# A memset behind each row gather in a graph kernel with four layers

## What is computed

```python
def _L0_gnn_ref(A, X, W, b):
    scores = jnp.where(mask, -jnp.arange(N), -inf)
    vals, idx = jax.lax.top_k(scores, S)            # S = 25: the first 25 neighbours
    feats = jnp.where(valid[..., None], X[idx], -inf)
    agg = feats.max(axis=2)
    agg = jnp.where((degree <= S)[..., None], jnp.maximum(agg, 0.0), agg)
    return relu(concatenate([X, agg]) @ W + b)

x = _layernorm(x + _L0(adj, x, ...))
x = _layernorm(x + _L1(x, adj, ...))     # graph attention, softmax over neighbours
x = _layernorm(x + _L2(x, adj, ...))     # the same again with other weights
x = _layernorm(x + _L3(x, adj, ...))     # dense attention, two steps with tanh
```

## Time and profile before

| | |
|---|---|
| timed runs, median of 3 | 1908.94 us (1906.79 to 1909.59) |
| profiled execution, span | 2892.8 us |
| TensorE matmul busy | 1713.1 us (59%) |
| TensorE weight load busy | 1233.8 us (43%) |
| VectorE busy | 1366.6 us (47%) |
| ScalarE busy | 937.2 us (32%) |
| GpSimd busy | 1263.5 us (44%) |
| mean granted TensorE clock | 0.773 of full speed |

### The profile page before, as it was taken

How to read it: one execution, slowest core, us unless ns; L and a number is a source line. 1 busy time by engine, 2 the same in 40 slices (tenths; PEclk the granted TensorE clock), 3 DMA queues, 4 the chain that set the end, 5 groups by cost and what they waited for, 6 DMA issues and landing times.

```text
span 2892.8 us, 27186 instructions
## 1 busy us (share of the span) xinstructions
PE 1713.1 (59%) x8580; PEld 1233.8 (43%) x8580; DVE 1366.6 (47%) x3417; ACT 937.2 (32%) x1311; POOL 1263.5 (44%) x1310
## 2 busy tenths in 40 slices
PE   1655767535765457664574655656455564756778
PEld 0543554424543245343452434434343343533655
DVE  3663664334743347443464434544354544443642
ACT  1010533323433324233332342223432325223223
POOL 5376344455344453444454443544435444255000
PEclk9987777767887668776697766877678776788789
DMA  4221212222222222222232221222312222121001
GB/s 126 61 74 43 71 51 90 55 77 62 59 77 61 66 62 61 77 71 55 58 85 62 70 77 29 80 70 70 77 38 71 70 69 63 36 67 52 23 15 37
DMA packets 160697, 182.18 MB, mean 63 GB/s; under 512 B 106397, under 2 KB 123690, under 8 KB 160554
## 3 DMA queue, kind: packets, MB, share of 16 engines
q1 hardware_dynamic: 119594, 96.43, 12.2%
q0 software_dynamic: 40960, 83.97, 10.8%
HBM read 155.66 MB, written 4.19 MB: 55 GB/s over the span
## 4 chain that ended last, share of the span: by engine, by line
PE 36%; another core or an unknown queue 24%; issue 18%; DVE 12%; ACT 5%; DVEq 4%; DMA 1%; SPq 1%; ACTq 0%
PE big L917 5%; PE spare L817 5%; PE side L1015 4%; PE big L1032 4%; PE big L986 4%; DVEq L69 3%; PE big L843 2%; PE big L999 2%; DVE probs_t L1327 2%; DVE pooled L1204 1%; PE big L817 1%; PE big L908 1%; PE big L864 1%; ACT adj_less L536 1%
## 5 line engine op out<-in xcount | busy, mean ns | idle before, releaser
L508 POOL DMA_INDIRECT gathered<-in_x_dram,rows x1280 | 1259.0, 984 | 1410.7 <-DVE pooled L1205 616.7
L817 PE MATMUL spare<-hot,x_part 128*128 128x512 f32 x1088 | 305.8, 427 | 86.9 <-issue 58.2
L917 PE MATMUL big<-values,probs_t 128*128 128x129 f32 x1792 | 254.0, 299 | 117.8 <-issue 117.0
L917 PEld LDWEIGHTS big<-values,probs_t 128*128 128x128 f32 x1792 | 241.8, 214 | 130.7 <-issue 125.7
L817 PEld LDWEIGHTS spare<-hot,x_part 128*128 128x128 f32 x1088 | 216.0, 203 | 150.5 <-issue 107.2
L1204 DVE TENSOR_REDUCE pooled<-gathered 128x128 f32<-128x2688 f32 (+1 forms) x56 | 253.0, 4517 | 6.4 <-issue 6.4
L986 PE MATMUL big<-probs_t,values 128*128 128x512 f32 x256 | 132.2, 666 | 160.4 <-issue 152.4
L1393 DVE TENSOR_REDUCE neg_max<-big 128x1 f32<-128x1024 f32 x64 | 78.3, 1223 | 286.2 <-remote 182.8
L1015 PE MATMUL side<-recip_diag,work 128*128 128x128 f32 x1024 | 143.6, 296 | 116.7 <-ACT probs_t L679 54.5
L1015 PEld LDWEIGHTS side<-recip_diag,work 128*128 128x128 f32 x1024 | 134.3, 208 | 146.6 <-issue 120.0
L563 ACT ACTIVATE hot<-running,minus_count 128x2048 fp32r<-128x2048 bf16 x84 | 167.4, 1993 | 58.9 <-remote 58.7
(11 more groups left out here) (191 smaller groups left out, 2642.0 us busy)
## 6 DMA issues: line engine op xcount, KB each, us to landing
adj_in<-in_adj_dram SPq DMA_DIRECT2D x128, 512.0 KB
gathered<-in_x_dram,rows POOLq DMA_INDIRECT x1280
xs<-in_x_dram SPq DMA_DIRECT2D x8, 512.0 KB
out_dram<-xs SPq DMA_DIRECT2D x8, 512.0 KB
adj_t<-adj_bf SPq DMA_TRANSPOSE x64
packed_t<-group_bits SPq DMA_TRANSPOSE x28
w_sb<-in_L_gnn_W_dram SPq DMA_DIRECT2D x1, 128.0 KB
w_sb<-in_L_gnn_W_dram SPq DMA_DIRECT2D x2, 64.0 KB
```

The costliest lines, as they stand in the source:

```text
L508: (late_gathered if late else rows_gathered[t % RING]).raised_by(pool.indirect_dma_start(out=gathered[:, t % RING, k * C:(k + 1) * C], out ...
L817: last = nc.tensor.matmul(pick_bank(b, q), x_parts[part][:, m, :], hot[c][:, m % per, :], start=(m == 0 and part == 0), stop=(m == T - 1 a ...
L917: last = nc.tensor.matmul(heads[:, t, 0:C + 1], probs_t[:, j, t * P:(t + 1) * P], values[:, j, :], start=False, stop=(j == T - 1), skip_gr ...
```

## The change

A new SBUF tile `pause` holds 6 x 256 bf16 elements on each partition. Behind each gather k of a tile GpSimd writes zeros to 256 elements on 32 partitions of it: partitions 0, 32, 64 or 96 onwards by k % 4, in column block k // 4, so that no two memsets of a tile touch the same place. The last memset of a tile raises a new semaphore, `paused`, and each tile but the first waits ahead of its gathers until the last memset of the tile before has been written. Nothing reads `pause`. There is no drain between a gather and its memset.

```diff
--- before.py
+++ after.py
@@ -30,6 +30,7 @@
 GATHERED = (21, 21)
 GATHERED_FIRST = 13
 LATE = 6
+PAUSE = 256
 PICKED = (SAMPLES - GATHERED[0], SAMPLES - GATHERED[1])
 PICKS = PICKED[0] + PICKED[1]
 BY_DVE = (PICKED[0], PICKED[0] + 1)
@@ -210,6 +211,7 @@
         row_f = sb("row_f", [P, 2, GATHERED[0]])
         rows = sb("rows", [P, T, GATHERED[0]], U32)
         gathered = sb("gathered", [P, RING, GATHERED[0] * C])
+        pause = sb("pause", [P, -(-GATHERED[0] // 4), PAUSE], BF16)
         running = sb("running", [P, T, N // 2], BF16)
         hot = [sb(f"hot{c}", [P, T // CHUNKS, N // 2], F32R) for c in range(CHUNKS)]
         x_parts = [sb(f"x_part{i}", [P, T, C], F32R) for i in range(X_PARTS)]
@@ -306,6 +308,7 @@
                                 first=ring_tiles(i, T) * GATHERED_FIRST - (i == late_ring) * LATE)
                          for i in range(RING)]
         late_gathered = signal("late_gathered", LATE, 16)
+        paused = signal("paused", T)
         gathers_begun = ctx.enter_context(nc.semaphore("gathers_begun"))
         loads_begun = ctx.enter_context(nc.semaphore("loads_begun"))
         rows_pooled = signal("rows_pooled", T)
@@ -495,6 +498,8 @@
                                         pattern=[[step, P]], channel_multiplier=-step).then_inc(consts, 1)
 
             def gather(b, t):
+                if t or not (isinstance(b, int) and b == 0):
+                    pool.wait_ge(paused.sem, paused.at(b, t))
                 if t % 2 == 0:
                     pool.wait_ge(rows_ready.sem, rows_ready.at(b, t // 2 + 1))
                 if t >= RING:
@@ -508,6 +513,9 @@
                     (late_gathered if late else rows_gathered[t % RING]).raised_by(pool.indirect_dma_start(
                         out=gathered[:, t % RING, k * C:(k + 1) * C], out_offset=None, in_=x_rows,
                         in_offset=bass.IndirectOffsetOnAxis(ap=rows[:, t, k:k + 1], axis=0)))
+                    quarter = k % 4 * 32
+                    last = nc.gpsimd.memset(pause[quarter:quarter + 32, k // 4, :], 0.0)
+                paused.raised_by(last)
 
             for t in range(T):
                 gather(0, t)
```

## The result

| | timed median | runs |
|---|---|---|
| kernel before | 1907.87 us | 1903.70 to 1909.59 |
| changed kernel | 2234.13 us | 2231.94 to 2235.16 |

The ratio is 1.171, with a 95% interval of 1.1688 to 1.1732: 326 us slower. The forecast was 2016 us (1959 to 2065 us as the case's own range), so the direction was right and the size was not: 107 us forecast, 326 us measured. The measured time lies in the wide range (1915 to 2260 us) and near the rival in which every memset costs its full length, 2214 us.

The account below looks back on a forecast made before the run. GpSimd was taken as all but the bound, TensorE's chain right beside it. 1908.9 + 122 (memsets) + 30 (borders) - 45 (slack) = 2016 us; likeliest case 1959 to 2065 us, wide range 1915 to 2260 us.

Parts of the forecast that it names:

- the case's own range: Bounds of the likeliest case, in which one memset in four costs its full length: 1959 to 2065 us, chance 0.45.
- The head of the page and the earlier trace: Profiled span of 2892.8 us against 1908.94 us timed: the extra 984 us are other engines' stalls while gathers run.
- The budget of GpSimd's idle time: Timed window for gathers, 1667 to 1706 us, leaves GpSimd 25 to 107 us idle; 45 us taken as absorbing work.
- The memset: 1280 memsets behind gathers: full length 0.25 us for one quarter, floor 0.033 us for the rest, 122 us in all.
- the quarter: In the memset's price: only memsets on partitions of the part preparing gathers, 368 of 1280, cost their full 0.25 us.
- the volume written: In the memset's price: 32 x 256 elements priced like 128 x 64, 0.087 us each, 111 us in all.
- The gap: The 0.30 us between gathers on GpSimd: claimed to be the engine's own execution, unable to hide a memset.
- the full-length rival: Every memset between gathers costs its full 0.25 us, 320 us in all: 2214 us (2157 to 2263), chance 0.25.
- The border: At each tile's start, the wait for GpSimd's last memset costs 0.6 us; 50 borders counted, 30 us (15 to 38).
- Collisions with VectorE: Memsets and gathers meeting VectorE's `hot` comparison hold each other up: set at nothing, bound some 10 us.
- What would prove me wrong: Gather step 1.28 us behind three memsets, 1.50 us behind the fourth; wrong on price if the step doesn't grow.
- The rival "faster": Thinner gather bursts relieve starved engines: 79 us back at most, 1830 us; a third gives 1883 us; chance 0.05.

Follow-up runs that it names:

- the border's wait alone: Kernel before plus one one-element memset behind a tile's last gather and the wait for it ahead of the next tile: 1933.6 us, 1.012.
- warm borders: Changed kernel with the border's wait raised by an earlier memset, so met beforehand: 2203.6 us, 1.155 of kernel before; 2327 us, 0.787, where that takes 2956 us.

## Why the prediction failed, step by step

**The head of the page and the earlier trace rows.** That the profiled execution lost its 984 us to stalls that the timed runs don't have was right, and the profile of the kernel before without stalls confirms it. I had left open why. The runs show that it goes with the chip, or with its state at the time, and not with the kernel; what stalls there isn't shown. The trace names no releaser for much of it: ScalarE's waits on something that the profile can't name are 631 us in the profile ahead of the prediction and 196 us in the one without stalls.

**The budget of GpSimd's idle time.** It gave 25 to 107 us for the window from the first gather on; measured are 30.6 us. Its two ends, 1667 and 1706 us for that window, hold the measured 1697 us. This step carried the sign of the forecast, and it held. I took 45 us of the idle time as able to absorb work, and 20 us of the first wait for pooling as able to absorb nothing; there are only 30.6 us, of which 28.9 us went in the change and 13 us in the run with the border's wait alone, and 1.7 us were left. Mis-sized by 16 us.

**The memset.** This is the step that failed. "If GpSimd's partitions are served by separate parts of it" gave 122 us; measured are 278.5 us. Two reasons stood for the low price, the quarter and the volume written, and the runs refute both: 1.276 us a step on the lower partitions, on the upper ones, and on all 128. The plain reading of the earlier trace rows, 0.25 us each and 320 us in all, was on the page, with the note that no row shows a memset made cheaper by fewer partitions. I let an account of how the engine is divided overrule the nearest rows. The rule that stood beside it, of the Trainium skill's GPSIMD Engine Reference, Instruction dispatch, and Perfetto Trace Analysis, DMA Instruction, SWDGE, would make three of four memsets cheap; the measurement decides against that reading. The pages don't say that a core skips a memset whose partitions are another core's; I added that.

**The gap.** "Can the 0.30 us gap hide it? I say no" was wrong in part. Behind a gather comes 0.04 us, the memset's span, and 0.16 us: 0.20 us of gap in place of 0.30 us. Some 0.10 us of a memset's span is hidden, so 256 elements (0.304 us) cost 0.204 us, 128 elements (0.198 us) cost 0.097 us, and one element (0.094 us) costs nothing. With this, the full-length rival's 320 us becomes 261 us. The kernels with 64 elements hide more: a span of 0.166 us costs 0.026 us, since the memset begins at the gather's end and not 0.04 us behind it. Those three kernels write the same partitions every time. In the others the 0.04 us is also gone exactly where two memsets in a row have the same quarter, at the first memset of 63 tiles; with warm borders, where no two do, it is never gone. So part of the price seems to belong to moving on to other partitions; no run tested that by itself.

**The border.** 0.6 us each was forecast, 30 us in all. The gap is 0.84 us in place of 0.16 us, 0.68 us each, and the waits for the memset are 47.8 us. Right in mechanism, 18 us short, or 9 us net of the 0.16 us that stand there anyway. By the runs its worth is 31 us in the changed kernel and 26 us alone.

**Collisions with VectorE.** "I set it at nothing; the bound is some 10 us." The gathers' busy time grew by 29.9 us, some 6 us of it because every gather takes 0.950 us in place of 0.945 us, the rest by collisions; the memsets' grew by about 18 us. GpSimd, then VectorE, in the changed kernel:

```profile
1044.69 0.30 POOL L517 MEMSET pause<- 32x256 bf16 x1
1045.15 1.89 POOL L513 DMA_INDIRECT gathered<-in_x_dram,rows  x1 [0.16 <-issue]
1047.08 0.30 POOL L517 MEMSET pause<- 32x256 bf16 x1
1047.55 1.89 POOL L513 DMA_INDIRECT gathered<-in_x_dram,rows  x1 [0.16 <-issue]
...
1043.74 8.46 DVE L1335 SCALAR_TENSOR_TENSOR probs_t<-row_gain,col_gain,adj_t 128x1024 f32<-128x1024 f32 x7
```

A gather beside VectorE's products of probabilities takes 1.89 us here in place of 0.95, and the next one again. Seven of those products take 8.46 us, 1.20 us from one to the next; the gathers then begin at 1045.15 and 1047.55, 2.40 us apart, so each meets the train at the same point of a product. I had looked only at the comparison of the earlier trace rows, and the trace puts the growth elsewhere: gathers held up beside L1327 of the kernel before are 13 with 8 us in all, beside the same line after (L1335) 52 with 42 us, while those beside the comparison are 48 us before and 42 us after. No memset is held up by the products, though 70 of them run beside one; 15 of the 19 memsets that take over 0.40 us stand beside the comparison. The Trainium skill (SBUF — State Buffer, Who interferes with whom) says that a VectorE instruction with two inputs in SBUF collides with a GpSimd instruction that reads SBUF and not with one that only writes it; this trace agrees, 52 gathers, which read `rows`, against no memset.

The step of 1.25 us had kept clear of these products. GpSimd, then VectorE, in the kernel before where it doesn't stall:

```profile
253.85 0.94 POOL L508 DMA_INDIRECT gathered<-in_x_dram,rows  x1 [0.30 <-issue]
255.10 0.94 POOL L508 DMA_INDIRECT gathered<-in_x_dram,rows  x1 [0.30 <-issue]
...
252.54 5.07 DVE L1327 SCALAR_TENSOR_TENSOR probs_t<-row_gain,col_gain,adj_t 128x1024 f32<-128x1024 f32 x4
```

There 86 of the 113 gathers that begin during a product begin in its first 0.1 us; none of these is held up, and 59 of the 112 steps from a product to the next take 1.24 us or more in place of 1.20, so it is VectorE that gives way. After the change no gather begins there: 56 begin during a product, most 0.2 us behind its start, and 52 are held up. Which of the two engines waits goes by the place in the product at which the gather begins.

**The sum.** 122 + 30 + 0 - 45 = 107 us was forecast; 278.5 + 47.8 + 29.9 - 28.9 = 327 us is what the rows give. Of the 220 us missing, 156 are the memset's (some 17 of them collisions), 30 the gathers' growth, 18 the border's and 16 the slack's. That the full-length rival came within 20 us is in part luck: it had the memsets 41 us too high, and the border, the slack and the collisions 64 us too low.

**What would prove me wrong.** "1.28 us behind three memsets and 1.50 us behind the fourth" is not what the profile shows: 1.454 us, whichever quarter the memset writes. That the profiled span is a poor judge was right in a way I hadn't seen: by 2892.8 against 2230.2 us the change looks faster by 23%, and by like against like it is slower by 17%. The rival "faster", by which the memsets relieve engines that the bursts starve, is what the form with warm borders does on the chip that stalls, by 629 us where I had allowed 79 us.

## What to carry to other kernels

When a profile and the timed runs differ by half, work the bound out from ends that don't depend on the stalls, and then get a profile from where the timed runs were made before comparing spans. Price an added instruction by the nearest rows of the same engine in full, take off only what a measured gap can hide (here 0.10 to 0.14 us of GpSimd's 0.30 us), and let no account of how an engine is built lower it without a row. On an engine that works from end to end, an added instruction costs its own time at each of its 1280 places, the restart behind each new wait, and what the new rhythm collides with.

## What the runs showed of the hardware that I had not expected

- On one chip the kernel before takes 2956 us, on others 1907 us, with the same gather step of 1.25 us. There the other engines stand still late in each burst of gathers. With memsets of 256 elements and a step of 1.458 us it takes 2327 us; with memsets of one element and a step of 1.252 us, 2903 us. Why it stalls there, whether it is the chip or its state at the time, and whether pace or memset relieves it, stays open.
- A GpSimd memset's price goes by the elements on one partition: 64 elements cost a step of 1.276 us on 32 lower, 32 upper or all 128 partitions.
- Between two gathers some 0.10 us of a memset is free, and 0.14 us where it writes the same partitions as the memset before it (64 elements).
- Gathers can fall into step with a train of VectorE instructions that come every 1.20 us and be held up one after the other, 1.89 us in place of 0.95 us; where they begin within 0.1 us of a VectorE instruction's start they are not held up, and VectorE's step grows from 1.20 to 1.25 us.
